# A two-layer hybrid network on one core: spike counts read from an SBUF copy, and another order of the side work in the 16-head attention

## The reference

```
# stages 1 and 3: y is compared with a membrane potential in five steps
h = square(relu(x @ W_fc.T));  y = h @ W_proj.T
mem = 0
for _ in range(5):
    mem_new = 0.9 * mem + y - (mem > 1);  spikes += (mem_new > 1);  mem = mem_new
out = spikes / 5
# stage 6: the softmax runs over the heads (axis 1), not over the keys
dp = einsum('bhqd,bhkd->bhqk', q, k) * 8 ** -0.5
attn = softmax(dp, axis=1)
out = einsum('bhqk,bhkd->bhqd', attn, v) -> (b, n, 128) @ w_proj + b_proj
```

## Time and profile before

| what | value |
|---|---|
| time, median of 3 runs | 2290.06 us (2285.96 to 2292.52) |
| the profiled execution | 2285.96 us, span 2284.2 us |
| mean granted TensorE clock | 0.919 |
| PE, DVE, ACT, POOL busy | 82%, 73%, 48%, 45% of the span |
| stage 6, halves of the attention | 1335.5 to about 1948 us, its last addition at 1963.9 us |

### The profile page before, as it was taken

One profiled execution on the slowest core, in us unless ns is written; L12 is line 12 of the kernel. 1 busy time (PEld: TensorE's weight loads), 2 busy tenths in 40 slices (PEclk: granted clock), 3 DMA queues, 4 the chain that ended last, 5 costly groups with the idle time before them and its releaser, 6 DMA issues.

```text
span 2284.2 us, 32109 instructions
## 1 busy us (share of the span) xinstructions
PE 1869.8 (82%) x12288; PEld 1210.5 (53%) x12288; DVE 1675.7 (73%) x2158; ACT 1107.3 (48%) x1830; POOL 1022.5 (45%) x382
## 2 busy tenths in 40 slices
PE   7988999854888885559999977788878777499998
PEld 5444444343444444447777754455555455377776
DVE  4655556255899985547777689999999999467666
ACT  2344445421634322115555566666676766355554
POOL 3476767411277750110000048788888999300000
PEclk8898999876999997669999999899999999699999
DMA  2112111000200000011010000000000000100000
GB/s 70 29 38 48 29 29 29 1 10 11 37 0 0 1 1 10 5 47 42 15 37 19 1 1 1 1 1 1 2 1 2 1 2 1 42 28 28 14 1 19
DMA packets 34014, 37.53 MB, mean 16 GB/s; under 512 B 5763, under 2 KB 21382, under 8 KB 33862
## 3 DMA queue, kind: packets, MB, share of 16 engines
q1 hardware_dynamic: 33334, 34.43, 6.0%
q10 hardware_dynamic: 528, 1.05, 0.2%
HBM read 19.48 MB, written 1.05 MB: 9 GB/s over the span
## 4 chain that ended last, share of the span: by engine, by line
PE 40%; issue 19%; DVE 19%; POOL 14%; ACT 4%; DMA 2%; SPq 1%; POOLq 0%; DVEq 0%; ACTq 0%; PEldq 0%
PE ps L46 9%; PE ps L47 8%; PE ps L48 7%; DVE negm L2122 7%; POOL AF L685 6%; POOL hc L1274 3%; POOL AF L1274 3%; PE ps L489 2%; PE ps L473 2%; PE ps L514 1%; DVE AF L2129 1%; PE ps L853 1%; POOL AR_plain L1982 1%; DVE AR L1063 1%; DVE AR L1057 1%
## 5 line engine op out<-in xcount | busy, mean ns | idle before, releaser
L1083 DVE TENSOR_TENSOR AF<-ps,AF 128x512 f32<-128x512 f32 x256 | 176.9, 691 | 182.8 <-ACT AF L1037 181.9
L2122 DVE TENSOR_REDUCE negm<-ps 128x64 bf16<-128x1024 f32 x256 | 302.4, 1220 | 11.3 <-PE ps L1999 11.2
L685 POOL TENSOR_TENSOR AF<-AF 128x2048 f32<-128x2048 f32 (+3 forms) x73 | 234.2, 3209 | 153.8 <-ACT AF L625 147.8
L46 PE MATMUL ps<-XH,AR 128*128 128x512 f32 x616 | 257.1, 417 | 35.1 <-DVE AF L894 18.1
L1037 ACT ACTIVATE AF<-ps 128x512 f32<-128x512 f32 x256 | 152.9, 597 | 260.6 <-PE ps L48 258.6
L1982 POOL TENSOR_TENSOR AR_plain<-AF 128x2048 f32<-128x2048 f32 x64 | 261.8, 4092 | 38.2 <-ACT AF L2076 37.4
L2096 ACT ACTIVATE AF<-ps 128x1024 f32<-128x1024 f32 x192 | 196.5, 1023 | 146.6 <-PE ps L2008 144.8
L47 PE MATMUL ps<-XL,AR 128*128 128x512 f32 x616 | 248.0, 403 | 0.0
L48 PE MATMUL ps<-XH,AR 128*128 128x512 f32 x616 | 247.3, 402 | 0.0
L2008 PE MATMUL ps<-negm,ident_bf 128*128 128x512 bf16 x512 | 161.0, 397 | 96.3 <-DVE negm L2122 96.1
L625 ACT ACTIVATE AF<-ps 128x512 f32<-128x512 f32 (+1 forms) x304 | 155.6, 576 | 146.0 <-PE ps L476 82.8
(11 more groups left out here) (309 smaller groups left out, 3948.2 us busy)
## 6 DMA issues: line engine op xcount, KB each, us to landing
AR<-AR SPq DMA_DIRECT2D x96, 128.0 KB, 2.4
AF<-in_L_ffn_Wg_dram SPq DMA_DIRECT2D x19, 256.0 KB, 2.7
AF<-in_L_ffn_Wu_dram SPq DMA_DIRECT2D x19, 256.0 KB, 3.0
AF<-in_L_ffn_Wd_dram SPq DMA_DIRECT2D x19, 256.0 KB, 3.8
AF<-AF SPq DMA_DIRECT2D x16, 64.0 KB, 2.4
AF<-AR_plain SPq DMA_DIRECT2D x16, 64.0 KB, 2.4
out_dram<-X SPq DMA_DIRECT2D x1, 1024.0 KB, 5.1
AF<-in_L_attn_a_Wq_dram SPq DMA_DIRECT2D x1, 512.0 KB, 4.0
```

Of the source, the lines that this page charges most:

```text
L46: pe.matmul(out, ah, bh, start=start, stop=False)
L685: pool.tensor_tensor(zacc[u % 2][:, :, c0:512], zacc[u % 2][:, :, c0:512], pt[t % 4][:, :, 0:w], ALU.add).then_inc(s0_zp, 1)
L1083: dve.tensor_tensor(mh[:, m % 3, :], bank(2 + m % 2), msg[:, m % 3, :], ALU.mult).then_inc(m_h, 1)
L2122: dve.tensor_reduce(negm6[:, j % 4, :], bank(2 * (j % 3), 2).rearrange("p (j q i) -> p q j i", j=HJ, i=2), mybir.AxisListType.XY, ALU.max, ...
```

## The change

It has two parts that have nothing to do with each other.

In stages 1 and 3, `spikes` first copies y from PSUM to a new SBUF tile `yv`, and the five comparisons read the copy. The semaphore that frees the PSUM bank (`s1_yc`) now fires after the copy.

In stage 6:

- the layernorm of the second batch moves to the front (statistics at j = 2 in one block, normalisation at j = 7 and 9, its two transposes are the first two jobs, at m = 4 and 6);
- the other jobs move by two places, keys and values go ahead of the queries of chunk 2, and the queries of chunk 3 start one group later;
- `project` stands behind the first tile of the next group instead of the second, and `add` behind that tile's sum over the heads;
- `flush` copies all four rows at once, and the four `scatter_part` instructions of a group stand together at m % 8 == 7, right behind the flush;
- two one-column tiles (`lo_q`, `lo_k`) move in SBUF, so that the tiles behind them start 8 bytes later;
- a wait in `make` is dropped, since its condition holds by then.

No instruction of stage 6 is added or removed; eight copies are added in stages 1 and 3.

```diff
@@ stages 1 and 3 @@
-                y, c = bank(4 + n % 2), cnt[:, i % 2, :]
+                y, c = yv[:, i % 2, :], cnt[:, i % 2, :]
+                dve.tensor_copy(y, bank(4 + n % 2)).then_inc(s1_yc, 1)
+                dve.wait_ge(s1_yc, n + 1)
                 link(dve.tensor_scalar(c, y, THR[0], None, ALU.is_gt))
-                for thr in THR[1:-1]:
+                for thr in THR[1:]:
                     link(dve.scalar_tensor_tensor(out=c, in0=y, scalar=thr, in1=c, op0=ALU.is_gt, op1=ALU.add))
-                dve.scalar_tensor_tensor(out=c, in0=y, scalar=THR[-1], in1=c, op0=ALU.is_gt,
-                                         op1=ALU.add).then_inc(s1_yc, 1)
-                dve.wait_ge(s1_yc, n + 1)
@@ stage 6: the tables @@
-        SPACED = q_jobs(1) + [("x", i) for i in (2, 3)] + q_jobs(2) + kv_jobs(1)
+        SPACED = ([("x", i) for i in (2, 3)] + q_jobs(1) + kv_jobs(1) + q_jobs(2))
         PLACED = [(job, LB * ((n + 1) // 3) + 2 * ((n + 1) % 3) + 2) for n, job in enumerate(SPACED)]
-        PLACED += [(job, LB * (8 + n // 3) + 2 * (n % 3) + 2) for n, job in enumerate(q_jobs(3))]
+        PLACED += [(job, LB * (9 + n // 3) + 2 * (n % 3) + 2) for n, job in enumerate(q_jobs(3))]
-        SCATTER_AT = {LB * (g - 2) + 2 * i: (g, i) for g in range(2, NB) for i in range(HS)}
+        SCATTER_AT = {LB * (g - 2) + 7: g for g in range(2, NB)}
@@ TensorE @@
-                    if kb == 1 and g:
+                    if kb == 0 and m:
                         project(g - 1)
@@ ScalarE @@
-                if j % 2 == 0 and m > 0 and m % LB == 0:
-                    flush(m // LB - 1, (2, 3))
                 if j % 2 and m >= 0:
                     if m % LB == LB - 1:
-                        flush(m // LB, (0, 1))
+                        flush(m // LB)
 ...
                     if m in SCATTER_AT:
-                        scatter_part(act, link, *SCATTER_AT[m])
+                        for i in range(HS):
+                            scatter_part(act, link, SCATTER_AT[m], i)
@@ VectorE @@
-                if j in (8, 10, 12, 14):
+                if j == 2:
                     dve.wait_ge(x_done, X_AFTER[s])
-                    ln_tiles_stats(dve, link, range(HB + j - 8, HB + j - 6))
-                if j == 16:
+                    ln_tiles_stats(dve, link, range(HB, NB))
+                if j == 4:
                     ln_half_aggr(dve, link, 1)
-                if j in (26, 28):
-                    ln_tiles_norm(dve, s, range(HB + 2 * (j - 26), HB + 2 * (j - 26) + 4))
-                m = j // 2 - LAG - 1
-                if j % 2 and m > LB and m % LB == 1:
-                    add(m // LB - 1)
+                if j == 7:
+                    ln_tiles_norm(dve, s, range(HB, HB + 4))
+                if j == 9:
+                    ln_tiles_norm(dve, s, range(HB + 4, NB))
                 if j % 2 and j >= 3:
                     denominators(j // 2 - 1)
+                    m = j // 2 - LAG - 1
+                    if m > 0 and m % LB == 0:
+                        add(m // LB - 1)
```

More of the change, by code:

```diff
@@ L784, in build @@
         cnt = tf(2, 512)
+        yv = tf(2, 512)
         fcT = [tr(FF * P), tr(FF * P)]
@@ L1720, in build @@
         bp6 = tf(D)
+        lo_q = tf(1)
+        lo_k = tf(1)
         hi6 = tf(2, 512)
@@ L1726, in build @@
         ot6 = tf(2, 512)
-        lo_q = tf(1)
-        lo_k = tf(1)
         k6 = [None, tr(SS, L)]
@@ L1773, in build @@
         FIRST = kv_jobs(0) + q_jobs(0)
-        SPACED = q_jobs(1) + [("x", i) for i in (2, 3)] + q_jobs(2) + kv_jobs(1)
+        SPACED = ([("x", i) for i in (2, 3)] + q_jobs(1) + kv_jobs(1) + q_jobs(2))
         PLACED = [(job, LB * ((n + 1) // 3) + 2 * ((n + 1) % 3) + 2) for n, job in enumerate(SPACED)]
-        PLACED += [(job, LB * (8 + n // 3) + 2 * (n % 3) + 2) for n, job in enumerate(q_jobs(3))]
-        JOBS = [(n, job, at) for n, (job, at) in enumerate(
-            [(job, None) for job in FIRST] + [x for x in PLACED if x[0][0] != "x"])]
+        PLACED += [(job, LB * (9 + n // 3) + 2 * (n % 3) + 2) for n, job in enumerate(q_jobs(3))]
+        JOBS = [(n, job, at) for n, (job, at) in enumerate([(job, None) for job in FIRST] + PLACED[2:])]
         JOBS_AT = {at: (n, job) for n, job, at in JOBS if at is not None}
-        LN_AT = {at: job[1] for job, at in PLACED if job[0] == "x"}
+        LN_AT = {at: job[1] for job, at in PLACED[:2]}
         MADE = {job: n for n, job, _ in JOBS}
-        SCATTER_AT = {LB * (g - 2) + 2 * i: (g, i) for g in range(2, NB) for i in range(HS)}
+        SCATTER_AT = {LB * (g - 2) + 7: g for g in range(2, NB)}
         def jobs_before(t):
@@ L1806, in make @@
             if at is not None:
-                pe.wait_ge(ln_lo, 4 * 6 + 2 + sum(1 for x in LN_AT if x < at))
                 pe.wait_ge(x_done, X_AFTER[6] + at // LB)
@@ L1976, in s6_pool @@
             pool.memset(ot6, 0.0).then_inc(s6_z, 1)
+            ln_half_rstd(pool, link, s, 1)
             for m in range(NTI):
-                if m == 7:
-                    ln_half_rstd(pool, link, s, 1)
                 pool.wait_ge(s6_wi, m + 1)
@@ L2026, in pv @@
                         wait(pe, s6_st, jobs_before(m))
-                        pe.wait_ge(ln_lo, 4 * s + 2 + sum(1 for at in LN_AT if at < m))
+                        pe.wait_ge(ln_lo, 4 * s + 2 + (2 if g else 0))
                         pe.wait_ge(x_done, X_AFTER[s] + max(g - 1, 0))
@@ L2037, in pv @@
                     ins.then_inc(s6_pv, 1)
-                    if kb == 1 and g:
+                    if kb == 0 and m:
                         project(g - 1)
                     if m in LN_AT:
-                        wait(pe, s6_st, jobs_before(m))
-                        pe.wait_ge(ln_lo, 4 * s + LN_AT[m])
-                        pe.wait_ge(x_done, X_AFTER[s] + m // LB)
+                        if LN_AT[m] == 2:
+                            pe.wait_ge(x_done, X_AFTER[s])
+                        else:
+                            pe.wait_ge(ln_lo, 4 * s + LN_AT[m])
                         ln_quarter_pe(pe, s, LN_AT[m], spare_bank(m))
@@ L2076, in invert, with flush @@
                 act.activation(w6i[:, m % 2, :], lnz, ACT.Exp, scale=-1.0).then_inc(s6_wi, 1)
[L2078 to L2084, removed]
+            def flush(g):
+                act.wait_ge(s6_pv, LB * (g + 1))
+                act.wait_ge(s6_z, 8)
+                wait(act, s6_o, g - 1)
+                for i in range(HS):
                     r = 32 * i
@@ L2087, in flush @@
                                    ACT.Copy).then_inc(chain_act if i < HS - 1 else s6_ot, 1)
-                    link.n += i < HS - 1
+                link.n += HS - 1
             for j in range(2 * NTI):
@@ L2111, in s6_act @@
                     if m in SCATTER_AT:
-                        scatter_part(act, link, *SCATTER_AT[m])
+                        for i in range(HS):
+                            scatter_part(act, link, SCATTER_AT[m], i)
             invert(NTI - 2)
             invert(NTI - 1)
-            flush(NB - 1, range(HS))
+            flush(NB - 1)
         def s6_dve(dve, link, s):
```

## The result

| what | before | after |
|---|---|---|
| time, median of the runs | 2289.01 us (4 runs, 2285.96 to 2292.52) | 2321.99 us (4 runs, 2319.38 to 2324.64) |
| ratio to before, 95% interval | | 1.0155 (1.0136 to 1.0174) |
| the profiled execution, its span | 2285.96, 2284.2 us | 2321.5, 2319.8 us |
| mean granted TensorE clock | 0.919 | 0.909 |
| first to last maximum of stage 6, starts | 1335.5 to 1942.0, 606.5 us | 1340.0 to 1977.4, 637.4 us |

Slower, by 33.0 us between the medians, where 33 was forecast (2323 us). The spans of the two profiled executions differ by 35.6 us, and stage 6 carries 30.9 us of that; by the ratio it would be 35.5 us.

The account below looks back on a forecast made before the run. VectorE was taken to bound stage 6, a ring of TensorE and VectorE stages 1 and 3. Idle 28.0 + 9.0 + 6.0 = 43.0 us against 14.4, plus 4.1, gave +32.7 us: 2323 us, 8-in-10 range 2302 to 2341.

Parts of the forecast that it names:

- Part one: `spikes`, stages 1 and 3: eight copies added, only the first comparison shortens, to 0.52 us; net 4.1 us, all on the path.
- Boundaries with a job: Stage 6, eight group boundaries (1 to 7, 10): VectorE idles 3.3 us each, boundary 7 1.6 us more; 28.0 us.
- The stack's stall hides the burst: Stage 6 job boundaries: TensorE is held anyway, so ScalarE's flushes, take and scatters make scores only 0.2 us later.
- Boundaries with a scatter but no job: Stage 6, boundaries 8, 9, 11 to 14: burst unhidden, 6 x 1.5 = 9.0 us; clock drops at half add 6 us.
- Costed at nothing: Stage 6: statistics and normalisation, among others, cost nothing; a badly met normalisation risks one GpSimd product (4.09 us) in two places.
- Rival 1: Stage 6: ScalarE's burst is mostly absorbed, +13 us, 2303 us; chance 0.20.
- Rival 2: Stage 6: GpSimd becomes late and TensorE waits for products at 7 late boundaries; +20 us, 2343 us; chance 0.12.
- Rival 3: Stage 6 gets faster: earlier `project` and `add` remove all 14.4 us idle; -10 us, 2280 us; chance 0.05.
- Rival 4: Only the `spikes` copies count, stage 6's new idle time equals the old; +4 us, 2294 us; chance 0.07.

Follow-up runs that it names:

- burst alone: Kernel before with only ScalarE's list changed: four flushes at once, four scatters behind them; table, `project` and layernorm as before; ratio 1.0122.
- early stack on part two: Part two of the change (old `spikes`) with jobs at m % 8 == 6 taken ahead of the flush and stacked behind the first maximum; ratio 1.0121 to before.
- burst and `project`: Kernel before with four flushes together, four scatters together, `project` and `add` one tile earlier; table and layernorm as before; ratio 1.0135.
- early stack: Kernel before with jobs at m % 8 == 6 taken ahead of the flush and stacked behind the next group's first maximum; ratio 0.9942, 2275.87 us.
- flushes alone: Kernel before with the four flushes together and scatters as before; ratio 1.0008.

## Why the prediction was right

**Part one, 4.1 us.** Right in kind: with two tensors nothing gets faster, as forecast (0.691 us before, 0.692 after). The first comparison was mis-sized: 0.427 us from SBUF where 0.52 was interpolated between a 128x1024 and a 128x128. So 3.4 us in the trace. The rule in the Trainium skill, "VectorE: DVE Perf Modes", "Rules for kernel authors", holds for one comparison of five here, and the row of the other four (691 ns) decides against it for this loop.

**Boundaries with a job, 28.0 us.** Measured 26.8 (1 to 7 and 10). The steps hold in kind: the scores 0.1 us later instead of 0.2, TensorE's 2.95 us unchanged, `project` at the low clock 1.76 and 0.48 us where up to 2.7 was allowed, the two halves behind it 0.47 and 0.35 us instead of 0.7 and 0.4. But the sum comes out better than its terms: boundaries 1 to 5 and 10 took 2.67 to 2.97 us where 3.3 was counted, boundary 6 took 3.99, and boundary 7 was put at 4.9 and took 5.98. At 6 and 7 the granted clock over the 7 us behind the gap was 0.51 and 0.50, at 1 to 5 0.67 to 0.68. "The stack's stall hides the burst" is shown by the run with the burst alone at boundaries 2 to 6, and from the other side by the early stack on part two.

**Boundaries with a scatter but no job, 9.0 + 6.0 us.** Measured 13.0. 1.5 us each at the three where the clock stays at 1.00 (9, 13, 14), as forecast. The other three (8, 11, 12) have 2.8 us: half of them drop, as assumed, but a drop costs 1.3 us and not 2.0.

**What was not in the sum.** In group 5 the jobs for values now stand where VectorE has no slack: 1.92 us. VectorE's busy time: L233 took 6.6 us instead of 5.5. Costed at nothing, with the lock named as a risk of one product in two places; the trace has it in one:

```profile
1356.72 5.46 DVE L233 TENSOR_SCALAR R<-X,mv,rstd 128x128 f32<-128x128 f32 x4
1358.02 4.08 POOL L1979 TENSOR_TENSOR AR_plain<-AF 128x2048 f32<-128x2048 f32 x1 [0.47 <-ACT AF L2074]
1365.56 1.04 PE L2005 MATMUL ps<-negm,ident_bf 128*128 128x512 bf16 x2 [6.88 <-DVE negm L2118]
```

The second four (1366.56) took 1.10 us, so most of it came back. TensorE's wait of 6.88 us cost VectorE nothing.

**The sum.** Idle of 41.8 us against a forecast of 43.0, less 14.4, is 27.4 us. The other 3.5 us of stage 6 are VectorE busy for longer, 595.6 against 592.1 us from the first to the last maximum: 1.1 us is L233, and the rest comes with the number of waits. Instructions in a row overlap a little. At boundary 3 the sum over the heads starts at 1492.54, while the maximum ahead of it, started at 1491.40 for 1.23 us, still runs for 0.09 us. An instruction that follows a wait has no such overlap. The kernel before has 12 waits of VectorE in stage 6, the changed one 41; 29 more at some 0.08 us are the 2.4 us that are left. The other runs agree: with 27 more waits (burst and `project`) 2.5 us, with 9 fewer (early stack) 1.0 us less, both without L233. The prediction counted idle time alone and had no term for this. With 3.4 us for `spikes` it makes 34.3 us by the terms, 35.6 between the spans, 33.0 between the medians. The errors of the terms (-0.7, -1.2, -2.0, +1.9, +3.5) are small and partly cancel; that the total came out within 1 us is in part luck.

**The rivals.** Rival 1 (burst absorbed) is true of the flushes alone and false of the whole (41.2 us idle before the maxima, not under 20). Rival 2 (GpSimd late): GpSimd does stand idle for ScalarE at a boundary (3.88 us before its product at 1698.86), but until the last products of the stage no idle time of VectorE or TensorE behind it shows. It is not far off: in both runs with the burst and the old table TensorE waits 2.29 us for a product at boundary 7. Rival 3 (stage 6 faster): the earlier `project` alone made it slower by 2 us of idle time and the lock. Rival 4 (only the copies count) asked for as much idle time as before, and there were 27.4 us more.

The weak place of the reasoning was not in the sum, but shows in the experiment with the burst alone: the 1.5 us for a boundary without a job held only since `project` had left the place where it would be waited for. As a price of the burst by itself it was too low by 0.85 us.

## What to carry to other kernels

An in-order queue between two engines has a lead, and work put into it in one piece is free up to that lead and paid beyond it: here the lead was 3.6 us, 2.4 us were free at all boundaries but one, 3.9 and 5.1 us were not. Price such a piece where nothing else holds the engines, since elsewhere a stall hides it; and when a stall hides something, ask whether the stall itself can go: here a side job placed two instructions earlier in VectorE's list (and ahead of the flush in ScalarE's) was worth 13 us.

## What the runs showed of the hardware

- A VectorE operation with one fp32 tensor (128x512) took 0.692 us from PSUM and 0.427 from SBUF; with two tensors 0.69 in either case. The copy out of PSUM took 0.692 us to save 0.265.
- VectorE's instructions in a row overlapped by some 0.08 us, and each wait in between cost that overlap too: 29 more waits made VectorE busy for 2.4 us longer with the same work.
- Four normalisations, 1.1 us together when undisturbed, took 5.46 us beside one product of GpSimd (one of them 4.1 us, as long as the product) and 8.73 beside two, and eight took between 2.6 us (early stack on part two) and 11.1 us (`project` alone) in kernels whose normalisations are the same instructions at other times. The Trainium skill, "SBUF — State Buffer", "Who interferes with whom", gives the rule of mutual exclusion for whole instructions; these rows agree with it, and show that a shift of some microseconds elsewhere can move it by 8 us, more than this kernel's measurement can tell from no change.
- After a gap of 2.93 to 2.95 us TensorE's clock was at its lower level for the whole of the next 7 us at some boundaries (0.50 at boundary 7) and for part of them at others (0.67, 0.77), and stayed at 1.00 at three with a gap of 2.92 to 2.94 us. What decides between them was not tried.
